# A four-layer sequence kernel: the routing's one-hot layout, its threshold step, one moved wait, and 39 and 143 expert tiles

## The reference

```
# layer 0: E = 8, one expert per token; each expert keeps its cap = T/8 = 512 likeliest tokens
probs = softmax(xt @ Wg)
_, top_idx = top_k(probs.T, cap)                      # per expert
masked = where(sel, probs.T, -inf)
tok2exp = where(assigned, argmax(masked), argmax(probs.T))
out += where(tok2exp == e, probs[tok2exp], 0) * (gelu(xt @ W1[e]) @ W2[e])
# layer 1: E = 16, four experts per token
topw, topi = top_k(softmax(x @ router_w + router_b), 4); topw /= sum(topw)
out = sum_e (gelu(x @ w1e + b1e) @ w2e + b2e) * combine[:, e]
```

## Time and profile before

| | us |
|---|---|
| median of 3 runs | 2050.89 |
| lowest, highest | 2049.95, 2053.34 |
| the profiled execution, its own time | 2053.53 |
| span of its instructions | 2051.8 |
| PE busy | 1673.2 (82%) |
| DVE busy | 1201.0 (59%) |
| ACT busy | 1083.9 (53%) |
| POOL busy | 613.3 (30%) |

### The profile page before, as it was taken

How to read it: one execution, slowest core, us unless ns; L and a number is a source line. 1 busy time by engine, 2 the same in 40 slices (tenths; PEclk the granted TensorE clock), 3 DMA queues, 4 the chain that set the end, 5 groups by cost and what they waited for, 6 DMA issues and landing times. The chain is left out here.

```text
span 2051.8 us, 33423 instructions
## 1 busy us (share of the span) xinstructions
PE 1673.2 (82%) x9958; PEld 1130.4 (55%) x9959; DVE 1201.0 (59%) x1940; ACT 1083.9 (53%) x2285; POOL 613.3 (30%) x562
## 2 busy tenths in 40 slices
PE   4988888562399879899999999932699999999990
PEld 1333333261299746444444444421599999999990
DVE  6999998486611154358999999268432332333224
ACT  6777776540033234137888888613355555555554
POOL 0000000000156322211222222100376767767760
PEclk9899999765599979989999999875799999999995
DMA  4000000124022096603333333075244444444417
GB/s 169 1 0 0 0 0 0 44 83 164 19 66 65 22 314 252 108 10 78 75 97 95 95 95 90 22 266 191 79 66 73 69 70 69 68 68 68 69 21 246
DMA packets 146024, 173.68 MB, mean 85 GB/s; under 512 B 29427, under 2 KB 110718, under 8 KB 145792
## 3 DMA queue, kind: packets, MB, share of 16 engines
q1 hardware_dynamic: 104160, 128.29, 20.5%
q0 software_dynamic: 33536, 43.71, 12.1%
q10 hardware_dynamic: 8224, 0.39, 0.2%
HBM read 111.77 MB, written 66.45 MB: 87 GB/s over the span
## 5 line engine op out<-in xcount | busy, mean ns | idle before, releaser
L1283 PEld LDWEIGHTS f_ht_ps<-f_XT,f_WS 128*128 128x128 f32 x2944 | 358.5, 193 | 15.8 <-DVE f_WS L1376 2.7
L1283 PE MATMUL f_ht_ps<-f_XT,f_WS 128*128 128x128 f32 x2944 | 361.7, 276 | 3.5 <-ACT f_XT L1324 3.5
L1291 PE MATMUL f_y_ps<-W,f_HT 128*128 x1472 | 347.9, 379 | 0.0
L2103 DVE TENSOR_REDUCE att_MX<-att_s_ps 128x2 f32<-128x1024 f32 x256 | 305.6, 1216 | 65.4 <-PE att_s_ps L1859 65.0
L1249 POOL DMA_INDIRECT moe<-f_Y,TOK x184 | 277.8, 1510 | 184.1 <-ACT f_Y L1349 156.3
L2066 ACT ACTIVATE att_PT<-att_st_ps 128x512 f32<-128x512 f32 x512 | 278.5, 595 | 74.7 <-PE att_st_ps L1884 66.7
L1291 PEld LDWEIGHTS f_y_ps<-W,f_HT 128*128 128x128 f32 x1472 | 265.5, 190 | 28.6
L1240 POOL DMA_INDIRECT XG<-x,TOK x184 | 193.8, 1053 | 232.2 <-issue 149.6
L1376 DVE COPY f_WS<-W 128x1024 f32 x184 | 131.6, 715 | 209.4 <-PE f_ht_ps L1283 128.7
L297 PE MATMUL rec_gate<-rec_XC,rec_W 128*128 128x512 f32 x384 | 189.6, 647 | 68.5 <-ACT rec_R L199 42.8
L1884 PE MATMUL att_st_ps<-att_Q,att_K 50*128 50x512 f32 x512 | 221.5, 488 | 19.6 <-ACT att_PT L2066 19.2
(11 more groups left out here) (265 smaller groups left out, 2230.3 us busy)
## 6 DMA issues: line engine op xcount, KB each, us to landing
W<-in_w SPq DMA_DIRECT2D x48, 512.0 KB, 9.8
att_Q<-qk_pairs SPq DMA_DIRECT2D x192, 64.0 KB, 2.8
att_K<-qk_pairs SPq DMA_DIRECT2D x192, 64.0 KB, 2.9
qk_pairs<-prj_HI SPq DMA_DIRECT2D x16, 512.0 KB, 3.8
qk_pairs<-prj_LO SPq DMA_DIRECT2D x16, 512.0 KB, 5.1
hidden<-in_xT SPq DMA_DIRECT2D x8, 512.0 KB, 7.9
x<-n_Y SPq DMA_DIRECT2D x8, 512.0 KB, 3.0
prj_X<-x SPq DMA_DIRECT2D x8, 512.0 KB, 8.7
```

What stands on the lines that cost most here:

```text
L1283: mm = nc.tensor.matmul(ht_ps[r % 2][:, f * P:(f + 1) * P], WS[r % 2][:, at:at + P], XT[r % 2][:, c], start=(c == 0), stop=(c == DC - 1))
L1291: mm = nc.tensor.matmul(y_ps[r % 2][:], HT[r % 2][:, f], W2[:, bass.ds(e * W_EXPERT + f * D, D)], start=(f == 0), stop=(f == FC - 1))
L2103: nc.vector.tensor_reduce(MX[n % 2][:, qc, :, p], s_ps[m % 2][:], AX.X, ALU.max).then_inc(s_mx, 1)
```

## The change

It has four parts. (1) The one-hots of a turn are laid out with the four slots innermost: `LOH` and `LTV` are [128, 128, 4], `HOH` [128, NT, 4]. They are compared with a new table `IOTA`, [128, max(128, NT), 4] in f16, in which each number stands four times, written by POOL at the start of the stage. The token's numbers exist in f16 too (`TVH`, K = 1). PE reads the operands of its products, `[:, :, r]`, with a step of four elements. (2) In the threshold search the next step's bits and the OR of `thr` are computed between the counting passes and the wait for PE; a step keeps `need3`, `pick1` and `cand` behind that wait. `cnt3` and a copy of `same` are in f16. (3) ACT's wait for the store of `CB` moves from in front of its turns to the end of its list. (4) `experts` runs 39 and 143 tiles; `route` keeps 40 and 144.

```diff
+def used_tiles(experts, choices):
+    return (T * choices - experts) // P + experts
@@ route, POOL
+            nc.gpsimd.iota(IOTA[:], [[1, WIDE], [0, SLOTS_AT_ONCE]], base=0, channel_multiplier=0,
+                           allow_small_or_imprecise_dtypes=True).then_inc(s_iota, 1)
@@ route, ACT
             act.dma_start(comb_out.rearrange("(j p) e -> p j e", p=P), CB[:]).then_inc(s_st, 16)
-            act.wait_ge(s_st, 16)
             if K > 1:
                 for g in range(TURNS):
...
+            act.wait_ge(s_st, 16)
@@ route, PE
-                    nc.tensor.matmul(cnt_ps[:, 0:3], C["same"][:], cnt3[:], start=True, stop=True).then_inc(s_count, 1)
+                    nc.tensor.matmul(cnt_ps[:, 0:3], same[:], cnt3[:], start=True, stop=True).then_inc(s_count, 1)
...
-                    mm = nc.tensor.matmul(tok_ps[:, 0:NT], LTV[g % 2][:, r], HOH[g % 2][:, r],
+                    mm = nc.tensor.matmul(tok_ps[:, 0:NT], LTV[g % 2][:, :, r], HOH[g % 2][:, :, r],
@@ route, DVE
+            if K == 1:
+                after(v.tensor_copy(TVH[:], TV[:]))
...
+                v.tensor_copy(same[:], C["same"][:])
                 after(v.memset(thr[:], 0))
                 for c in range(3):
-                    after(v.memset(bits[:, c:c + 1], (c + 1) << (BITS - 2)))
+                    after(v.memset(bits[0][:, c:c + 1], (c + 1) << (BITS - 2)))
+                    after(v.memset(cand[:, c:c + 1], (c + 1) << (BITS - 2)))
...
                 for i in range(BITS // 2):
-                    after(v.tensor_tensor(cand[:], thr[:].to_broadcast([P, 3]), bits[:], ALU.bitwise_or))
                     for c in range(3):
                         ins = v.tensor_scalar(above[c][:], PRT[:], cand[:].bitcast(F32)[:, c:c + 1], None, ALU.is_ge, ALU.add,
                                               accum_out=cnt3[:, c:c + 1])
-                    counted(ins)
+                    step[0] += 1
+                    ins.then_inc(s_mask, 1)
+                    now, then = bits[i % 2], bits[(i + 1) % 2]
+                    if i >= 1:
+                        after(v.tensor_tensor(thr[:], thr[:], pick1[:], ALU.bitwise_or))
+                    if i < BITS // 2 - 1:
+                        after(v.tensor_scalar(then[:], now[:], 2, None, ALU.logical_shift_right))
+                        after(v.tensor_tensor(under[:], thr[:].to_broadcast([P, 3]), then[:], ALU.bitwise_or))
+                    dve.wait_ge(s_count, step[0])
                     after(v.tensor_scalar(need3[:], cnt_ps[:, 0:3], float(CAP), None, ALU.is_ge, ALU.add, accum_out=need1[:]))
-                    after(v.tensor_tensor(pick1[:], need1[:], bits[:, 0:1], ALU.mult))
-                    after(v.tensor_tensor(thr[:], thr[:], pick1[:], ALU.bitwise_or))
-                    after(v.tensor_scalar(bits[:], bits[:], 2, None, ALU.logical_shift_right))
+                    after(v.tensor_tensor(pick1[:], need1[:], now[:, 0:1], ALU.mult))
+                    if i < BITS // 2 - 1:
+                        after(v.tensor_tensor(cand[:], pick1[:].to_broadcast([P, 3]), under[:], ALU.bitwise_or))
+                after(v.tensor_tensor(thr[:], thr[:], pick1[:], ALU.bitwise_or))
...
+            dve.wait_ge(s_iota, 1)
+            wide, low = [P, NT, SLOTS_AT_ONCE], [P, P, SLOTS_AT_ONCE]
             for g in range(TURNS):
...
-                ins = v.tensor_tensor(LOH[g % 2][:], C["iota16"][:, 0:P].unsqueeze(1).to_broadcast(low), lo.to_broadcast(low),
-                                      ALU.is_equal)
+                hi, lo = (t[:, at].unsqueeze(1) for t in (HI, LO))
+                ins = v.tensor_tensor(LOH[g % 2][:], IOTA[:, 0:P], lo.to_broadcast(low), ALU.is_equal)
...
-                    v.tensor_tensor(LTV[g % 2][:], LOH[g % 2][:], TV[:, at].unsqueeze(2).to_broadcast(low), ALU.mult).then_inc(s_ltv, 1)
+                    v.tensor_tensor(LTV[g % 2][:], LOH[g % 2][:], TVH[:, at].unsqueeze(1).to_broadcast(low), ALU.mult).then_inc(s_ltv, 1)
...
-                v.tensor_tensor(HOH[g % 2][:], C["iota16"][:, 0:NT].unsqueeze(1).to_broadcast(wide), hi.to_broadcast(wide),
-                                ALU.is_equal).then_inc(s_oh, 1)
+                v.tensor_tensor(HOH[g % 2][:], IOTA[:, 0:NT], hi.to_broadcast(wide), ALU.is_equal).then_inc(s_oh, 1)
@@ experts
-    NT = slot_tiles(E, K)
+    NT = used_tiles(E, K)
     R = len(XG)
+    LAPS = -(-NT // R)
+    LAST = NT - (LAPS - 1) * R
```

More of the change, by code:

```diff
@@ L866, in route @@
             thr = st.sb("thr", [P, 1], I32)
-            bits = st.sb("bits", [P, 3], I32)
+            bits = [st.sb(f"bits{k}", [P, 3], I32) for k in range(2)]
+            under = st.sb("under", [P, 3], I32)
             cand = st.sb("cand", [P, 3], I32)
@@ L873, in route @@
             EQT = st.sb("EQT", [P, 2 * P])
-            cnt3 = st.sb("cnt3", [P, 3])
+            cnt3 = st.sb("cnt3", [P, 3], F16)
+            same = st.sb("same", [P, P], F16)
             need3 = st.sb("need3", [P, 3])
@@ L883, in route @@
         onesE = st.sb("onesE", [P, E])
[L884 to L888, removed]
+        SI = st.sb("SI", [P, TILES * K], I32)
+        LO_I = st.sb("LO_I", [P, TILES * K], I32)
+        HI_I = st.sb("HI_I", [P, TILES * K], I32)
+        LO = st.sb("LO", [P, TILES * K], F16)
+        HI = st.sb("HI", [P, TILES * K], F16)
+        WIDE = max(P, NT)
+        IOTA = st.sb("IOTA", [P, WIDE, SLOTS_AT_ONCE], F16)
+        TVH = st.sb("TVH", [P, TILES], F16)
         AT = st.sb("AT", [P, TILES])
         TV = st.sb("TV", [P, TILES])
-        SF = st.sb("SF", [P, K, TILES])
+        SF = st.sb("SF", [P, TILES * K])
         own_end = st.sb("own_end", [E, E])
@@ L896, in route @@
         UP = st.sb("UP", [P, NT])
-        LOH = [st.sb(f"LOH{h}", [P, SLOTS_AT_ONCE, P], F16) for h in range(2)]
-        LTV = [st.sb(f"LTV{h}", [P, SLOTS_AT_ONCE, P], F16) for h in range(2)]
-        HOH = [st.sb(f"HOH{h}", [P, SLOTS_AT_ONCE, NT], F16) for h in range(2)]
+        LOH = [st.sb(f"LOH{h}", [P, P, SLOTS_AT_ONCE], F16) for h in range(2)]
+        LTV = [st.sb(f"LTV{h}", [P, P, SLOTS_AT_ONCE], F16) for h in range(2)]
+        HOH = [st.sb(f"HOH{h}", [P, NT, SLOTS_AT_ONCE], F16) for h in range(2)]
         cnt_ps = st.ps("cnt_ps")
@@ L913, in route @@
         s_set = st.sem("patterns_set")
+        s_iota = st.sem("slot_numbers_ready")
         s_sub = st.sem("shifted")
@@ L1137, in _ @@
                 after(v.tensor_tensor(A[:], RANK[:], OH[k][:], ALU.mult))
-                after(v.tensor_reduce(SF[:, k], A[:].rearrange("p e j -> p j e"), AX.X, ALU.add))
+                after(v.tensor_reduce(SF[:].rearrange("p (j k) -> p j k", k=K)[:, :, k], A[:].rearrange("p e j -> p j e"), AX.X, ALU.add))
             after(v.tensor_copy(SI[:], SF[:]))
@@ L1152, in _ @@
                 at = slice(g * SLOTS_AT_ONCE, (g + 1) * SLOTS_AT_ONCE)
-                hi, lo = (t[:, 0, at].unsqueeze(2) if K == 1 else t[:, :, g:g + 1] for t in (HI, LO))
-                wide, low = [P, SLOTS_AT_ONCE, NT], [P, SLOTS_AT_ONCE, P]
-                ins = v.tensor_tensor(LOH[g % 2][:], C["iota16"][:, 0:P].unsqueeze(1).to_broadcast(low), lo.to_broadcast(low),
-                                      ALU.is_equal)
+                hi, lo = (t[:, at].unsqueeze(1) for t in (HI, LO))
+                ins = v.tensor_tensor(LOH[g % 2][:], IOTA[:, 0:P], lo.to_broadcast(low), ALU.is_equal)
                 if K == 1:
                     after(ins)
-                    v.tensor_tensor(LTV[g % 2][:], LOH[g % 2][:], TV[:, at].unsqueeze(2).to_broadcast(low), ALU.mult).then_inc(s_ltv, 1)
+                    v.tensor_tensor(LTV[g % 2][:], LOH[g % 2][:], TVH[:, at].unsqueeze(1).to_broadcast(low), ALU.mult).then_inc(s_ltv, 1)
                 else:
                     ins.then_inc(s_loh, 1)
-                v.tensor_tensor(HOH[g % 2][:], C["iota16"][:, 0:NT].unsqueeze(1).to_broadcast(wide), hi.to_broadcast(wide),
-                                ALU.is_equal).then_inc(s_oh, 1)
+                v.tensor_tensor(HOH[g % 2][:], IOTA[:, 0:NT], hi.to_broadcast(wide), ALU.is_equal).then_inc(s_oh, 1)
                 if g == 1:
@@ L1261, in _ @@
             for r in range(R):
-                pool.wait_ge(s_sc[r], 16 * NT // R)
+                pool.wait_ge(s_sc[r], 16 * len(range(r, NT, R)))
         @block.tensor
@@ L1299, in lap @@
             def lap(g, last=False):
-                for r in range(R):
+                for r in range(LAST if last else R):
                     n = g * R + r
                     e = expert_of(n)
-                    if not (last and r == R - 1):
+                    if not (last and r == LAST - 1):
                         hidden(n + 1, (r + 1) % R)
-                    if not (last and r >= R - 2):
+                    if not (last and r >= LAST - 2):
                         x_transposes(n + 2, (r + 2) % R, g if r < R - 2 else g + 1)
@@ L1309, in _ @@
             lap(0)
-            with pe.Fori(1, NT // R - 1) as g:
+            with pe.Fori(1, LAPS - 1) as g:
                 lap(g)
```

(10 more changed lines are left out.)

## The result

The changed kernel takes 2025.99 us (median of 4 runs, 2023.18 to 2028.56) where the kernel before took 2052.11 beside it (median of 4, 2049.95 to 2053.50): ratio 0.9873, 95% interval 0.9854 to 0.9893, or 22 to 30 us less. I had forecast 35.3 less, 2015.6, with a range that ended at 2026. The profiled execution took 2028.56 and spans 2026.8, so the two profiles differ by 25.0.

What follows compares the result with a forecast made beforehand. DVE was taken to bound the routers' search and turns, PE the expert stages. Search -8.1, first turns -4.9, second turns -14.8 and tiles -7.5 gave -35.3 us, from 2050.89 to 2015.6, range 2009 to 2026.

Steps and rivals of the forecast that it cites:

- The search: First router's threshold search: steps fall from 2.96 to 2.40 us, 44.2 to 35.9 in all (-8.3); whole term -8.1.
- The turns of the first router: First router's one-hot turns: DVE at doubled 16-bit pace, 1.57 to 0.96 us a turn, -4.9 us over eight.
- The turns of the second router: Second router's one-hot turns: 5.6 us stall goes, then a two-buffer round of 2.00 us per two turns binds; -14.8 us.
- no change: PE's f16 products in the turns: reading operands in steps of 8 bytes leaves their 0.11 to 0.12 us each.
- PE pays for the steps: Rival, turns of both routers: 0.23 us a product, costing 6.6 us in the second; total -28.4, 2022.5 us; chance 0.12.
- The prediction's sentence from the Trainium skill: PE's operand reads: 16-byte lines carry no penalty up to a step of 8 bf16 elements; a step of four lies inside.
- The tiles: Both expert stages: one tile fewer each at 3.73 us a tile, the tail staying; -7.5 us.
- less than 1 us in a stage in which POOL is idle: Start of each router: `IOTA` is one POOL instruction of under 1 us, needed 70 and 50 us later.
- The sum: Whole kernel: -8.1 - 4.9 - 14.8 - 7.5 = -35.3 us, median 2050.89 to 2015.6.
- As every stage ends before the next begins, a gain in a stage goes whole into the span: Whole kernel: stage gains count fully, unless a load that ran under the stage becomes late; no size given.
- the clock rises in r1: Rival, second router's turns: at 2.4 GHz the round is 1.76 us, -3.8, f1's first products -1.5; 2010.5 us; chance 0.15.

Runs made afterwards that it cites:

- e3: Kernel before with only the new one-hot layout, the table and 16-bit `TVH`, the store's wait left in place: median 2041.72 us, ratio 0.9945.
- e4: Kernel before with only ACT's wait for the store of `CB` moved behind the turns: median 2044.74 us, ratio 0.9968.
- e8: Changed kernel with three sets of `LOH`, `LTV` and `HOH` in place of two: median 2013.99 us, ratio to the kernel before 0.9814.
- e1: Kernel before with only the expert tile counts changed, 39 and 143 in place of 40 and 144: median 2046.4 us, ratio 0.9963.
- e7: Changed kernel with POOL's table made later, after DVE's subtraction of the maximum: median 2021.19 us, ratio to the kernel before 0.9854.
- e14: Changed kernel with three sets of one-hot buffers and POOL's table made later: median 2012.64 us, ratio to the kernel before 0.9798.
- e15: e14 plus two products that nothing reads, in TensorE's idle time before the attention's last relative-part transposes: median 2012.0 us, ratio to the kernel before 0.9804.

## Why the prediction was wrong

- *The search*: -8.60 for -8.3 from the first pass to `SELT`. Right, by the mechanism forecast: a step of 2.38 for 2.40, with PE's product at 0.19, shorter than the half to two thirds of 0.59 that I had taken, and hidden.
- *The turns of the first router*: -4.91 for -4.9. Right.
- *The turns of the second router*: -14.05 for -14.8. The mechanism was right, as `e3`, `e4` and `e8` show: a stall of 5.6, then the round over two buffers. The term was mis-sized by 0.05 a round, 0.75 in all, and that is what the step of four elements costs PE: a group of four products takes 0.68 in place of 0.64. My "no change" for it was wrong, and the rival "PE pays for the steps", at 6.6 us, was wrong by far more. `e3`, with the new layout, has the 0.68 as well, and `e4`, with the old one, the 0.64; the last group, beside which DVE and ACT are idle, takes 0.68 too. The prediction's sentence from the Trainium skill has no penalty for such a step; the trace shows this small one.
- *The tiles*: -7.5 forecast; -7.2 in `e1`, which has them alone. Right.
- *`IOTA`*: "less than 1 us in a stage in which POOL is idle", at no cost. It took 1.20 and 1.33, and made `AT` wait for its end. It cost 0.95 in the first router and 0.8 in the second, where the start was 0.42 longer in all, part of it having been a wait for the bias. `e7` shows this.
- *The sum.* With the measured terms, starts +1.0 and +0.4, search -8.6, turns -4.9 and -14.05, tiles -3.6 and -3.6, it is -33.4, 2 short of mine. The step that failed is "As every stage ends before the next begins, a gain in a stage goes whole into the span". The stages hang together through TensorE's clock. In the profiled pair the attention gave back 6.8 us and the first experts some 2.3 (351.48 - 3.6 = 347.9, measured 350.10); over the three profiles of the changed kernel and two of the one before it is 5.5 (mean 448.4 against 442.8) and 1.8 (349.65 against 351.5 - 3.6). From -33.4 that leads to -26.1, which is what the medians differ by.

That it is the clock is shown: the windows are alike until it rises, the length of the low stretch follows the place of the fall in fifteen profiles, and a delay of 0.67 us, in a stage 350 us earlier, shortens it from 27 to 31 us to 20.5. The delay saves 4 us of time, of which some 2 come from this stretch and the rest from the earlier rise in the first experts. For the first experts' share the kernels with 39 tiles speak: the stretch takes 347.85 to 347.87 where the clock rises after 4.1 us (`e1`, `e7`, `e14`) and 349.4 to 350.1 where it rises after 9.8 to 10.0. That no edit as such causes the long stretches is shown as well, since the delayed kernel has them all. My rival "the clock rises in r1" looked at the clock, but at the stage that I was changing. What decides where in the work the clock falls, and why a shift of less than 0.1 us there moves the rise by 14 us, stays open. The Trainium skill, "TensorE: Matmul & The Clock Gate", Part 1, says that the chip watches activity without regard to where the kernel is, so that the point of a rise varies with it; the trace agrees in kind, but the page puts the variation at half a microsecond, and here low stretches over the same work differ by up to 14 us. The price is up to 7 us in one place. It also holds such ramps to be under 1% of a span, which is true of these 7 of 2027 us, but they were a fifth of the expected gain.

## What to carry to other kernels

Before adding up gains of stages, look for stretches at half clock behind the stages that move: each is a term with an uncertainty of its own, here 17 to 31 us long and worth some 0.4 to 0.7 us for each microsecond, and it belongs in the range whatever the edits do. When a stage without a changed line is longer, compare its windows from a common marker until the counts part; and test with a delay, which should cost its own length if nothing depends on when the work falls. When a faster engine brings forth a wait over two buffers, price a third buffer at once: it was worth 9.4 us of the turns here.

## What the runs showed of the hardware

- A POOL iota of 1.20 us held a DVE tensor_scalar of 128x32 f32 for 1.13 us in place of 0.18, while a DVE reduction (0.42) and a reciprocal (0.35) beside the same iota kept their times. The Trainium skill, "GPSIMD Engine Reference", section 1, has the two engines share their way into the buffer and contend for some kinds of DVE instruction; the trace agrees, and shows the hold to last as long as the POOL instruction does.
- TensorE ran at 0.50 for up to 30.7 us while busy in 15.74 of the last 16 us of it; in other kernels the clock rose after 17.1 us of the same work. It fell in the changed kernel behind 5 us with the engine busy in 2.79 of them, and in `e15` behind 5 us with 4.18.
- f16 products whose two operands are read in steps of 8 bytes took a little longer than in steps of 2: 21.9 us in place of 20.4 for 128 products of 144 columns at 0.50, and 0.34 in place of 0.31 to 0.32 for four of 40 columns.
